# Attention kernel on one core: eight of sixteen exchange transfers per piece issued by ScalarE instead of four

## What is computed

```python
xn = layernorm(x)
q  = (xn @ wq.T) per head -> q_nope (128), q_pe (64, rotated)
kv = xn @ wkv_a.T         -> kv_lat (128, rms-normed = kv_cache), k_pe (64, rotated)
q_lat  = q_nope @ wkv_b[:, :128]                  # per head, into the latent
scores = (q_lat @ kv_cache.T + q_pe @ k_pe.T) * SCALE, causal mask
attn   = softmax(scores)
out    = ((attn @ kv_cache) @ wkv_b[:, 128:].T) @ wo.T
return x + out + ternary_linear(xn) + bias
```

## Time and profile before

| what | us |
| --- | --- |
| median of 3 runs | 1756.08 (1755.11 to 1757.51) |
| the profiled execution | 1750.59 |
| span of its trace | 1748.8 |
| TensorE busy in the span | 1657.4 (95%) |
| VectorE, ScalarE, GpSimd busy | 1179.8 (67%), 819.9 (47%), 963.6 (55%) |
| mean granted TensorE clock, share of full speed | 0.986 |

### The profile page before, as it was taken

One profiled execution on the slowest core, in us unless ns is written; L12 is line 12 of the kernel. 1 busy time (PEld: TensorE's weight loads), 2 busy tenths in 40 slices (PEclk: granted clock), 3 DMA queues, 4 the chain that ended last, 5 costly groups with the idle time before them and its releaser, 6 DMA issues. The chain is left out here.

```text
span 1748.8 us, 27070 instructions
## 1 busy us (share of the span) xinstructions
PE 1657.4 (95%) x9030; PEld 1395.1 (80%) x9030; DVE 1179.8 (67%) x2755; ACT 819.9 (47%) x1295; POOL 963.6 (55%) x595
## 2 busy tenths in 40 slices
PE   6889999889999998999999999999999999999996
PEld 5667777677777777888888888888888888888885
DVE  6546777676677766667766776667767677677663
ACT  4434445344554444354444555444454544544452
POOL 4663444435555554565655656556665565646554
PEclk9899999999999999999999999999999999999998
DMA  7848887667666666565555555656656465655553
GB/s 287 321 174 240 277 259 233 214 165 197 175 157 157 157 179 195 156 200 155 147 158 154 159 151 157 199 145 192 169 131 166 118 163 149 157 139 142 148 128 102
DMA packets 117375, 309.08 MB, mean 177 GB/s; under 512 B 28786, under 2 KB 29299, under 8 KB 115956
## 3 DMA queue, kind: packets, MB, share of 16 engines
q1 hardware_dynamic: 89008, 227.04, 45.2%
q10 hardware_dynamic: 28228, 80.31, 16.7%
HBM read 113.25 MB, written 34.60 MB: 85 GB/s over the span
## 5 line engine op out<-in xcount | busy, mean ns | idle before, releaser
L1458 POOL TENSOR_TENSOR pT<-pT,pT_h 128x1024 fp32r<-128x1024 f32 x320 | 689.2, 2183 | 421.3 <-ACT pT_h L1349 418.9
L1211 DVE TENSOR_SCALAR_CACHE_REDUCE probs<-p_score 128x512 f32<-128x512 f32 (+3 forms) x640 | 380.8, 601 | 334.9 <-PE p_score L1138 217.3
L1328 ACT ACTIVATE probs<-probs,neg_max 128x128 f32<-128x128 f32 (+15 forms) x256 | 307.4, 1201 | 406.3 <-DVE neg_max L1217 329.1
L1349 ACT ACTIVATE pT_h<-pT 128x1024 fp32r<-128x1024 f32 x320 | 291.3, 963 | 228.2 <-PE p_out L1158 171.3
L1233 DVE STREAM_TRANSPOSE turned<-probs 128x1024 f32<-128x1024 f32 (+7 forms) x384 | 341.5, 915 | 41.7 <-ACT probs L1328 36.6
L1158 PE MATMUL p_out<-pT_h,V_h 128*128 128x256 f32 (+3 forms) x1024 | 300.5, 293 | 11.6 <-POOL pT L1458 11.3
L1158 PE MATMUL p_out<-pT,V_h 128*128 128x256 f32 (+3 forms) x1024 | 303.3, 296 | 0.0
L1158 PE MATMUL p_out<-pT_h,V_l 128*128 128x256 f32 (+3 forms) x1024 | 303.0, 296 | 0.0
L1138 PE MATMUL p_score<-Kp,qp_h 128*128 128x512 f32 (+3 forms) x640 | 236.3, 369 | 11.5 <-POOL qp_l L1450 11.2
L1138 PE MATMUL p_score<-Kn_h,q_h 128*128 128x512 f32 (+3 forms) x640 | 243.1, 380 | 2.2 <-PEq L272 1.6
L1138 PE MATMUL p_score<-Kn_l,q_h 128*128 128x512 f32 (+3 forms) x640 | 234.0, 366 | 0.0
(11 more groups left out here) (131 smaller groups left out, 2098.0 us busy)
## 6 DMA issues: line engine op xcount, KB each, us to landing
pT<-turned SPq DMA_DIRECT2D x384, 128.0 KB, 3.3
Wq<-wq_scr ACTq DMA_DIRECT2D x63, 512.0 KB, 4.4
Wv<-wv_scr SPq DMA_DIRECT2D x63, 512.0 KB, 4.0
pT<-turned SPq DMA_DIRECT2D x192, 112.0 KB, 3.8
pT<-turned SPq DMA_DIRECT2D x192, 96.0 KB, 2.5
pT<-turned ACTq DMA_DIRECT2D x128, 128.0 KB, 3.9
Wp<-wp_scr SPq DMA_DIRECT2D x31, 512.0 KB, 4.8
pT<-turned SPq DMA_DIRECT2D x192, 80.0 KB, 2.8
```

What stands on the lines that cost most here:

```text
L1211: dve.tensor_scalar(probs[row % ROW_RING][:, b * CW:b * CW + width], p_score[n % SCORE_RING][:, 0:width], SCALE, LOWEST, ALU.mult, ALU.max ...
L1328: act.activation(probs[row % ROW_RING][:, 0:width], probs[row % ROW_RING][:, 0:width], ACT.Exp, bias=neg_max[p][:, i:i + 1], scale=1.0, ac ...
L1349: act.activation(high.rearrange("p r t i q -> p r t (i q)"), low.bitcast(F32).rearrange("p r t i q -> p r t (i q)"), ACT.Copy).then_inc(p_ ...
L1458: pool.tensor_tensor(low.rearrange("p r t i q -> p r t (i q)"), low.bitcast(F32).rearrange("p r t i q -> p r t (i q)"), high.bitcast(F32). ...
```

## The change

For pieces of chunks three and four, SyncE no longer issues quarter 2, and ScalarE issues quarters 2 and 3, in this order, at the place where it issued quarter 3. Waits, semaphores and sizes stay.

```diff
                 if new == 1:
                     store_half(new - 1, 1)
                     load_residual(new, 0)
-                if 1 <= s <= SLOTS:
+                if 1 <= s <= SLOTS and phase(s - 1) < 2:
                     exchange(s - 1, (2,))
@@ exchange_last on ScalarE @@
-                for r in range(4):
-                    act.dma_start(slots(pT[s % 2][96:P, :], s)[:, r, 0:tiles, :, :].bitcast(F32),
-                                  slots(turned[s % 2][32 * r:32 * (r + 1), :], s)[:, 3, 0:tiles, :, :]
-                                  ).then_inc(exchanged[s % 2], 16)
+                for a in (2, 3) if phase(s) >= 2 else (3,):
+                    for r in range(4):
+                        act.dma_start(slots(pT[s % 2][32 * a:32 * (a + 1), :], s)[:, r, 0:tiles, :, :].bitcast(F32),
+                                      slots(turned[s % 2][32 * r:32 * (r + 1), :], s)[:, a, 0:tiles, :, :]
+                                      ).then_inc(exchanged[s % 2], 16)
```

## The result

The changed kernel takes 1803.03 us (median of 4 runs, 1799.85 to 1807.15) against 1755.59 us of the kernel before measured beside it (1749.09 to 1757.51): a ratio of 1.027, 95% interval 1.024 to 1.030. That is 47 us more, where 26 were forecast; the measured time lies above the stated range, which ended at 1800. The profiled execution's span is 1800.4 us.

A forecast was written before the change was run, and what follows sets the result against it. TensorE was taken as the bound, with 13.9 us idle in the middle stretches; chunk four's 14.7 plus chunk three's 12.3 minus 1.0 at the end gave +26.0 us, a median of 1782, range 1758 to 1800.

The forecast's parts named there:

- the signs that were named: Changed profile: eight issues of 5 to 7 us, exponential behind issuing above 150 us, `o_l` waits some 25, idle about 40.
- Price of an issue: ScalarE's four extra issues per piece: 2.5 us in chunk three, 3.4 opening and 3.1 closing in chunk four.
- The prediction's upper bound: At 1 us an issue, 4 us per slot: about 4.3 us a pair in chunk four, chunk three 23 us; +54, 1810.
- The clock: Rival, chance 0.14: chunk three's waits grow to 3 us and lower TensorE's clock, 7 times, 15 us more: 1797.
- Two heads of each pair: Chunk four: one head's closing slot starts 0.32 us late, costing 1.13; the other's on time, 0.81; 1.94 us a pair.
- I cost it at nothing: Chunk four: the fourth group's low part is late but still before its product; 1 us per closing slot if wrong.
- Chunk three: Closing slots: late `q_h` delays `o_l` and TensorE's projection, 1.5 us in five pairs, 2.4 in two: 12.3 us.
- SyncE's shorter list at zero: SyncE loses four issues, some 3 us per piece; pieces land sooner, but that was costed at zero in the middle.
- The end: After the last tile, the last piece's exchange is issued sooner by eight and eight: a gain of 1.0 us.
- Absorbed: Rival, chance 0.10: issuing beside queued work and VectorE's idle time take up the extra issues: about 1756.
- Faster by earlier landing: Rival, chance 0.06: late landing was TensorE's real wait and SyncE's shorter list cures it: 1750.4.
- The page's rule: Queues share the same 16 DMA engines; more issuers save only sequencer time, usually small: the sum would be near nothing.

## Why the prediction was right in kind and wrong in size

- **The path: right.** ScalarE's issuing, the exponential and `q_h` behind it, VectorE's `q_l`, copies and maximum, `o_l`, and TensorE's projection. Each shows in the rows above, and moving the issues alone (1.001) removes the loss. Most of the signs that were named came: eight and eight issues, 155.9 us behind issuing, 36.9 us for `o_l` (25 had been named), idle time of 46 us (40 had been named). One did not: eight issues were to take 5 to 7 us, and in opening slots of chunk four they took 7.7.
- **The step that failed in chunk four: "Price of an issue".** It was bounded at 1 us an issue, and the value was taken from the kernel before, 3.4 and 3.1 us for four more, because SyncE's later issues ran at 0.79 us. But those ran after ScalarE had stopped; with both queues at it for all eight, the extra was 7.6 - 3.4 = 4.2 us in an opening and 6.7 - 3.1 = 3.6 us in a closing slot. The prediction's own working with these: the opening slot passes on 4.2 - 2.42 - 0.66 = 1.1 us, a closing slot costs 3.6 - 0.8 - 1.49 = 1.3 us, a pair 2 x 1.3 + 1.1 = 3.7 us against 3.7 measured on average and 1.94 forecast. That makes 7 x 3.7 + 1.3 = 27.2 us where 14.7 were forecast and 32.5 measured. Behind 2.3 us of slack, 0.5 to 0.8 us on the price doubled the loss. The prediction's upper bound, 1 us an issue, had given 4.3 us a pair, and so was nearer than the value taken; it had also given 1810 us, and the stated range stopped at 1800 all the same.
- **The clock: left out of the sum.** It was priced as a rival, at seven falls of 2.2 us in chunk three. Four came, two of them in chunk three, at 1.7 us each, 6.7 us. They stand behind waits of 1.6 to 3.4 us; at 877.68 us one of 1.68 us brought none, so the length of the wait alone does not tell where.
- **What was missing, added up (an estimate).** Of the 25.6 us between the forecast's 26.0 and the 51.6 of the profiled executions, the price makes 12.5, the falls of the clock 6.7, the wait of scores for `q_l` 2.0 and the smaller gain at the end 0.6; 3.8 us stay open.
- **Two heads of each pair: right.** The one closing slot starts late, the other on time; closing slots alone cost 2.7 us in the pair shown, as 2 x 1.3 says.
- **"I cost it at nothing", the fourth group: wrong as a wait, right as a cost.** TensorE does wait 14.4 us for it (weight loads), but taking that wait away gains nothing.
- **Chunk three: the waits right, the sum too small, 12.3 against 19.6 us.** The price was nearly as forecast, 5.3 us for eight in most closing slots, 2.6 more than before, up to 6.5 with a slow issue. The waits of the projection for `o_l` came as forecast, one in each pair: seven of 1.44 to 1.68 us and one more of 0.73, 12.6 us by the weight loads. (2.4 us in two of them, as the forecast had it, was not seen.) Beside them stand two falls of the clock, 3.4 us, and a second door that the forecast had not: the scores of the next head also wait for `q_l` (0.8 us at 872.86 in the changed kernel), 2.0 us in all. Some 2 us stay open. By pairs, the six from head three to fourteen took 1.7 to 3.3 us each, 14.6 together.
- **Chunk four's first head: not in the sum.** It was counted as a common one. It cost 4.5 us; one wait of TensorE for `o_l` there is 3.4 us, where 1.2 stood before, and one of the falls of the clock stands behind it. Why the wait is so long was not tried.
- **SyncE's shorter list at zero: right.** A transfer of 128 KB by SyncE takes a little longer to land (median 3.8 us behind its issue from 1203 to 1700 us, 3.0 before), one of 112 KB a little less (3.5, 3.9 before), but the list is shorter, and the late landings are gone, with no gain. The end gave 0.4 us, not 1.0: ScalarE's longer issuing held up the fourth group of the piece before, and so `o_h`, by part of the same microsecond.
- **The rivals.** Absorbed: it holds for six and ten (1.003) and for opening slots (1.003), not for eight in closing ones. Faster by earlier landing: its mechanism took place and was worth nothing. Slower by the clock: its time, 1797, is nearest to the measured one, and its mechanism did occur, but it explains 6.7 us and not the rest; that its number lies so near is luck. The page's rule (the Trainium skill, DMA: Bandwidth & Descriptors, Issuing engines are not separate DMA queues) held in its first half: the two queues share what carries the bytes, as halving the bytes shows. In its second half, that the time to issue is usually small, it does not help here: one issue takes 0.6 to 0.95 us where a transfer lands 3 to 4 us behind its issue, but eight in a row take 5.3 to 7.7 us, more than that.

## What to carry to other kernels

An engine that is half idle can still have no time at the place where it is asked to issue: read from its timeline what stands behind the issue in its own order, and put the issue behind the work that others wait for. Price an issue with the traffic that the change itself makes, both queues at once, not by the median of before; and where the cost is what is left above a slack, carry the whole range of the price through, since small errors in it double the result. Two waits of one engine are one loss if the same chain is late at both, so a new wait in the list is no proof that removing it pays.

## What the runs showed of the hardware

The time for which a queue is held by one exchange transfer depended on what else was being moved, eight in a row: 0.63 us with no exchange transfers on the other queue (128 KB each) and about 0.66 us with both queues at it and 64 KB each, but 0.95 us with both and 128 KB each. At that pace sixteen transfers of 128 KB go out in 7.6 us, about 275 GB/s (an estimate from these rows). That the queue which issues is held by the bytes of the other one had not been in the forecast.

TensorE's granted clock can fall to the lower of its two levels behind a short wait: in four places of the changed kernel, behind waits of 1.64, 1.68, 2.42 and 3.39 us, about 1.7 us were lost each time, while five other waits of 1.44 to 1.68 us in chunk three were followed by none.
